# A vision tower with routed experts on one core: routed rows added to the output in memory, four late blocks worked between the units

## The reference, cut to what matters

```python
h = h + conv(layernorm(h))                      # residual h, 12608 tokens x 192
x = layernorm(h)
probs = softmax(x @ router_w)                   # 8 experts
gates, idx = top_k(probs, 2); gates /= sum(gates)
g = silu(x @ w_gate[e]);  u = x @ w_up[e]       # expert e, hidden width 192
routed = sum over the token's two experts of gate * ((g * u) @ w_down[e])
shared = (silu(x @ ws_gate) * (x @ ws_up)) @ ws_down     # hidden width 768
alpha = sigmoid(x @ sg_w + sg_b)
out = h + alpha * shared + (1 - alpha) * routed
```

## Time and profile before

| | us |
|---|---|
| median of 3 runs | 1256.18 (1250.46 to 1256.38) |
| the profiled execution | 1252.63 |
| its span, first to last instruction | 1250.80 |
| shared stage, first chunk to the next stage | 326.5 to 777 |
| units, first matmul to the last scatter | 782.4 to 1137.4 |
| `finish`, first transfer to the end | 1147.0 to 1250.8 |

### The profile page before, as it was taken

One profiled execution on the slowest core, in us unless ns is written; L12 is line 12 of the kernel. 1 busy time (PEld: TensorE's weight loads), 2 busy tenths in 40 slices (PEclk: granted clock), 3 DMA queues, 4 the chain that ended last, 5 costly groups with the idle time before them and its releaser, 6 DMA issues. The chain is left out here.

```text
span 1250.8 us, 24364 instructions
## 1 busy us (share of the span) xinstructions
PE 1040.9 (83%) x7867; PEld 718.1 (57%) x7868; DVE 868.9 (69%) x2637; ACT 537.4 (43%) x1023; POOL 656.7 (53%) x682
## 2 busy tenths in 40 slices
PE   5977997684599998999999996888878878864997
PEld 5967886684365655656666663444444445432555
DVE  6999776322487788888788765566666666651998
ACT  1233533222455555555556541444444444431332
POOL 0134413000377776777777752376766776763543
PEclk9989999788699999999999998899999999996999
DMA  8678786866995435454333216565555555333997
GB/s 298 239 238 268 231 257 161 212 132 172 203 211 148 123 90 135 121 129 97 93 87 97 69 49 184 117 126 111 129 113 118 123 115 135 94 86 112 306 299 241
DMA packets 285967, 196.08 MB, mean 157 GB/s; under 512 B 178840, under 2 KB 264602, under 8 KB 285590
## 3 DMA queue, kind: packets, MB, share of 16 engines
q1 hardware_dynamic: 251152, 142.46, 44.6%
q0 software_dynamic: 19488, 39.17, 9.3%
q10 hardware_dynamic: 15206, 12.93, 4.0%
HBM read 100.52 MB, written 74.65 MB: 140 GB/s over the span
## 5 line engine op out<-in xcount | busy, mean ns | idle before, releaser
L1728 POOL DMA_INDIRECT parts<-unit_yu,unit_token x208 | 215.9, 1038 | 97.2 <-issue 47.4
L1310 POOL DMA_INDIRECT routed<-rows_w,slot x198 | 216.6, 1094 | 64.1 <-issue 64.1
L1492 DVE SCALAR_TENSOR_TENSOR hf<-psu,sg 128x512 f32<-128x512 f32 x120 | 82.8, 690 | 83.8 <-ACT sg L1233 40.3
L1160 PE MATMUL pso<-ffn_w_hi,hh 128*128 128x192 f16 x480 | 119.4, 249 | 23.0 <-DVE hl L1497 18.0
L1233 ACT ACTIVATE sg<-psg 128x512 f32<-128x512 f32 x120 | 71.8, 599 | 147.3 <-PE psg L1145 114.2
L454 POOL TENSOR_TENSOR e_rs<-e_ve,mhalf 98x8 f32<-98x8 f32 x16 | 49.8, 3114 | 138.3 <-DVE e_ve L692 131.4
L1160 PE MATMUL pso<-ffn_w_hi,hl 128*128 128x192 f16 x480 | 119.2, 248 | 0.3 <-issue 0.3
L1160 PE MATMUL pso<-ffn_w_lo,hh 128*128 128x192 f16 x480 | 119.1, 248 | 0.0
L1145 PE MATMUL psg<-xt,ffn_w_hi 128*128 128x512 f16 x360 | 118.9, 385 | 0.0
L1145 PE MATMUL psu<-xt,ffn_w_hi 128*128 128x512 f16 x360 | 118.0, 382 | 0.3 <-issue 0.3
L524 PE MATMUL ps<-w,area 128*98 128x192 f32 x528 | 99.9, 333 | 0.0
(11 more groups left out here) (245 smaller groups left out, 2817.9 us busy)
## 6 DMA issues: line engine op xcount, KB each, us to landing
end_part<-parts SPq DMA_DIRECT2D x48, 384.0 KB, 5.6
area<-in_xa_dram SPq DMA_DIRECT2D x33, 392.0 KB, 5.5
area<-in_xb_dram SPq DMA_DIRECT2D x33, 392.0 KB, 6.2
resid<-spare ACTq DMA_DIRECT2D x32, 294.0 KB
hin<-resid SPq DMA_DIRECT2D x24, 384.0 KB
yin<-mixed SPq DMA_DIRECT2D x96, 96.0 KB
spare<-in_xa_dram SPq DMA_DIRECT2D x15, 392.0 KB, 6.1
spare<-in_xb_dram SPq DMA_DIRECT2D x15, 392.0 KB, 7.6
```

What stands on the lines that cost most here:

```text
L1160: last = nc.tensor.matmul(o, hx[m % 2][:, ts], wd[k][:, m], start=(a == 0 and m == 0 and t % 2 == 0), stop=(a == 2 and m == NSH - 1), skip ...
L1310: nc.gpsimd.indirect_dma_start(out=routed[:, :], out_offset=bass.IndirectOffsetOnAxis(ap=slot[q][:, k, t:t + 1], axis=0), in_=rows_w[q][:, ...
L1492: nc.vector.scalar_tensor_tensor(out=hf[i][:], in0=psu[:, i], scalar=1.0 / SCALE, in1=sg[i][:], op0=ALU.mult, op1=ALU.mult).then_inc(s["hf ...
L1728: nc.gpsimd.indirect_dma_start(out=parts[:, :], out_offset=bass.IndirectOffsetOnAxis(ap=token[q][:, k:k + 1], axis=0), in_=y[q][:, k, :], ...
```

## The change

- `NLATE` is 4: 21 blocks get their shared part in `shared_expert`, 126 chunks, and `PACE` is 5 for each period and 6 for the last.
- The last four blocks' chunks are worked in `routed_experts` as 48 half chunks (256 tokens, 128 hidden columns), one "guest" with each of the 48 written-out units: `guest_up` between `up(i)` and `down(i-1)`, `guest_down` after `down(i-1)`. Their results stay in `sums`.
- `lay`: SP stores each block's `sums` to `out` during `shared_expert` (for the four late blocks the residual alone). 14 of these stores stand between the loads, 10 after them, the last (block 20) after the fillers.
- A unit's indirect DMAs go to `out` itself with an add. Rows of one expert's units never meet; rows of two experts can. So `unit_table` makes a third row of `units`: the number of the first unit of this unit's expert, plus one. SP counts units whose rows have landed (`landed`), after the load of the unit five further on, and `send` waits for the count that the table gives. The first send also waits for all `lay` stores.
- After the last unit GpSimd adds the four late blocks from `sums` to `out` with five plain DMAs that add. `parts` and `finish` are gone, and with them one of two small operations of `meta`.

```diff
--- before.py
+++ after.py
@@ -85,13 +85,20 @@
...
-NLATE = 5
+NLATE = 4
+HOSTED = 4
 NOW = NBLK - NLATE
-PACE = [5, 5, 4] * ((NBLK - 1) // 3) + [8]
+LATE = NOW + HOSTED
+PACE = [5] * (NBLK - 1) + [6]
 XR = 8
 MAX_UNITS = 2 * NTOK // UNIT + E
 MIN_UNITS = -(-2 * NTOK // UNIT)
 STRAIGHT = MIN_UNITS - 2
+HALVES = 2 * HOSTED
+GUESTS = NSH * HALVES
+GUEST_OF = {i: i for i in range(GUESTS)}
+NLAID = NBLK + 1
+HB = BT // 2
...
@@ -1068,6 +1078,22 @@
...
+            def lay(b):
+
+                if b < NOW:
+                    sp.wait_ge(s["out_ready"], 2 * (b + 1))
+                else:
+                    sp.wait_ge(s["h2_ready"], b + 1)
+                sums = sums_of(t, b, tiles(b))
+                if b < NBLK - 1:
+                    sp.dma_start(rows(out, b, NT), sums).then_inc(late["laid"], 16)
+                else:
+                    at = (NBLK - 1) * BT
+                    mid = LAST_START + 128
+                    sp.dma_start(out[at:mid], sums[at - LAST_START:128, 0]).then_inc(late["laid"], 16)
+                    sp.dma_start(out[mid:NTOK].rearrange("(t p) d -> p t d", p=128),
+                                 sums[:, 1:]).then_inc(late["laid"], 16)
...
@@ -1083,7 +1109,13 @@
...
+                if LAG <= b < LAG + EASY:
+                    lay(b - LAG)
+
+            for b in range(NOW, NBLK):
+                lay(b)
+            for b in range(EASY, NOW - 1):
+                lay(b)
...
@@ -1095,6 +1127,7 @@
...
+            lay(NOW - 1)
             sp.wait_ge(s["fillers"], 16 * (NFILL + 1 + E))
...
@@ -1469,6 +1502,9 @@
...
+                step(nc.vector.tensor_tensor(gj[:], ge[:], start[:].unsqueeze(1).to_broadcast(shape), ALU.mult))
+                step(nc.vector.tensor_reduce(firstf, gj[:], op=ALU.max, axis=X))
+                nc.vector.tensor_scalar(t["units"][:, 2], firstf, 1.0, None, ALU.add)
...
@@ -1609,8 +1651,18 @@
...
+        def guest(i):
+
+            return GUEST_OF.get(i) if isinstance(i, int) else None
+
+        def guest_place(j):
+
+            half, m = divmod(j, NSH)
+            b, side = NOW + half // 2, half % 2
+            return b, side, m, min(NT // 2, tiles(b) - side * NT // 2)
...
@@ -1630,7 +1682,31 @@
...
-            schedule(n, sp, load)
+            def land(q, value):
+
+                sp.wait_ge(s[f"sent{q}"], value)
+                sp.sem_inc(late["landed"], 1)
+
+            def sent_by(i):
+
+                return 32 * (i - i % 2) + 64
+
+            sp.sem_inc(late["landed"], 1)
+            for i in range(STRAIGHT):
+                load(i, i % 2, i % XB, 16 * (i // XB + 1))
+                if i >= BEHIND:
+                    land((i - BEHIND) % 2, sent_by(i - BEHIND))
+            land((STRAIGHT - BEHIND) % 2, sent_by(STRAIGHT - BEHIND))
+            with nc.sync.Fori(0, n - STRAIGHT // 2) as j:
+                for i in range(2):
+                    load(2 * j + (STRAIGHT + i), i, i, None)
+                for i in range(2):
+                    land(i, 64 * j + sent_by(STRAIGHT - 4))
+            more = nc.sync.value_load(t["pairs"][0:1, 0:1], min_val=MIN_UNITS // 2 - 1, max_val=(MAX_UNITS + 1) // 2 - 1)
+            for i in range(2):
+                land(i, 64 * more)
+            for i in range(2):
+                land(i, 64 * n)
...
@@ -1670,12 +1746,41 @@
...
+            def guest_up(j):
+                b, side, m, nt = guest_place(j)
+                cols, ts = slice(m * 128, (m + 1) * 128), slice(side * HB, side * HB + nt * 128)
+                if j >= 2:
+                    pe.wait_ge(late["hf_ready"], j - 1)
+                for k in range(2):
+                    prods = ((wa[0], 0), (wa[1], 0), (wa[0], 2), (wb[0], 1), (wb[1], 1))
+                    for a, (wt, x) in enumerate(prods):
+                        last = nc.tensor.matmul(gps[:, j % 2, k * HB:k * HB + nt * 128], wt[:, k, cols],
+                                                t["xt"][b % XR][:, x, ts], start=(a == 0), stop=(a == 4))
+                last.then_inc(late["g_ps"], 1)
+
+            def guest_down(j):
+                b, side, m, nt = guest_place(j)
+                pe.wait_ge(late["hl_ready"], j + 1)
+                if m == 0 and j:
+                    pe.wait_ge(late["out_ready"], j // NSH)
+                for k in range(nt):
+                    for a, (hx, r) in enumerate(((hhx, 0), (hhx, 1), (hlx, 0))):
+                        last = nc.tensor.matmul(gpo[:, k * D:(k + 1) * D], hx[j % 2][:, k * 128:(k + 1) * 128],
+                                                wd[r][:, m], start=(a == 0 and m == 0 and k == 0),
+                                                stop=(a == 2 and m == NSH - 1), skip_group_check=True)
+                last.then_inc(late["down_ps"], 1)
+
             def body(i, q, k, landed):
                 up(i, k, landed)
+                if guest(i) is not None:
+                    guest_up(guest(i))
                 if not (isinstance(i, int) and i == 0):
                     down(i - 1, 1 - q)
+                if isinstance(i, int) and guest(i - 1) is not None:
+                    guest_down(guest(i - 1))
 
             schedule(n, pe, body)
...
@@ -1703,8 +1808,21 @@
...
+                j = guest(i)
+                if j is not None:
+                    act.wait_ge(late["g_ps"], j + 1)
+                    if j >= 2:
+                        act.wait_ge(late["hf_ready"], j - 1)
+                    nj = guest_place(j)[3] * 128
+                    nc.scalar.activation(sgx[j % 2][:, 0:nj], gps[:, j % 2, 0:nj], ACT.Silu,
+                                         scale=1.0 / SCALE).then_inc(late["sg_ready"], 1)
                 if not (isinstance(i, int) and i == 0):
                     y_out(i - 1, 1 - q)
+                if j is not None:
+                    act.wait_ge(late["hf_ready"], j + 1)
+                    if j >= 2:
+                        act.wait_ge(late["down_ps"], j - 1)
+                    nc.scalar.copy(hhx[j % 2][:, 0:nj], hfx[j % 2][:, 0:nj]).then_inc(late["hh_ready"], 1)
...
@@ -1718,6 +1836,9 @@
...
                 pool.wait_ge(s["y_d"], i + 1)
+                if isinstance(i, int) and i == 0:
+                    pool.wait_ge(late["laid"], 16 * NLAID)
+                pool.wait_ge(late["landed"], table(nc.gpsimd, 2, i))
...
@@ -1726,13 +1847,12 @@
...
                     nc.gpsimd.indirect_dma_start(
-                        out=parts[:, :], out_offset=bass.IndirectOffsetOnAxis(ap=token[q][:, k:k + 1], axis=0),
-                        in_=y[q][:, k, :], in_offset=None, bounds_check=2 * NTOK - 1,
-                        oob_is_err=False).then_inc(s[f"sent{q}"], 16)
+                        out=out[:, :], out_offset=bass.IndirectOffsetOnAxis(ap=token[q][:, k:k + 1], axis=0),
+                        in_=y[q][:, k, :], in_offset=None, bounds_check=NTOK - 1,
+                        oob_is_err=False, compute_op=ALU.add).then_inc(s[f"sent{q}"], 16)
 
             nc.gpsimd.memset(const[:], 0.0).then_inc(s["const_ready"], 1)
-            nc.gpsimd.memset(span[:], float(NTOK)).then_inc(s["const_ready"], 1)
-            pool.wait_ge(s["const_ready"], 2)
+            pool.wait_ge(s["const_ready"], 1)
...
@@ -1740,8 +1860,21 @@
...
             send(2 * n - 1, 1)
-            for q in range(2):
-                pool.wait_ge(s[f"sent{q}"], 64 * n)
+            pool.wait_ge(late["landed"], 2 * n + 1)
+            pool.wait_ge(late["out_ready"], HALVES)
+            wait(pool, "turn", 2 * n)
+            nc.gpsimd.tensor_tensor(carry[:], const[:], const[:], ALU.add).then_inc(s["turn"], 1)
+            for b in range(NOW, NBLK):
+                sums, at = sums_of(t, b, tiles(b)), b * BT
+                if b == NBLK - 1:
+                    mid = LAST_START + 128
+                    nc.gpsimd.dma_start(out[at:mid], sums[at - LAST_START:128, 0],
+                                        accum_op=ALU.add).then_inc(late["added"], 16)
+                    sums, at = sums[:, 1:], mid
+                end = min(NTOK, (b + 1) * BT)
+                nc.gpsimd.dma_start(out[at:end].rearrange("(t p) d -> p t d", p=128), sums,
+                                    accum_op=ALU.add).then_inc(late["added"], 16)
+            pool.wait_ge(late["added"], 16 * (HOSTED + 1))
...
@@ -1753,16 +1886,13 @@
...
-                nc.vector.scalar_tensor_tensor(out=shift[:].unsqueeze(2), in0=first, scalar=expert,
-                                               in1=span[:].unsqueeze(2), op0=ALU.is_equal,
-                                               op1=ALU.mult).then_inc(s["parts_ready"], 1)
...
-                dve.wait_ge(s["parts_ready"], 2 * i + 2)
...
-                nc.vector.tensor_tensor(token[q][:].unsqueeze(2), shift[:].unsqueeze(2), word[:, :, 0:1], ALU.add)
+                nc.vector.tensor_copy(token[q][:].unsqueeze(2), word[:, :, 0:1])
...
@@ -1775,8 +1905,20 @@
...
+            def guest_out(j):
+                b, side, m, nt = guest_place(j)
+                if m < NSH - 1:
+                    return
```

(42 more changed lines are left out.)

170 lines of the change are left out of this document (10 added, 160 removed).

## The result

The changed kernel takes 1246.25 us (median of 12 runs, 1241.63 to 1250.59), the kernel before in the same session 1253.66 (12 runs, 1247.94 to 1258.08): ratio 0.9952, interval 0.9934 to 0.9970. That is 7 us or 0.5% faster, where 1213, 3.2% less, was forecast. The forecast is 33 us too low.

The account below looks back on a forecast made before the run. The prediction took TensorE to bound the shared stage, the units' engines to wait for each other, and DMA and TensorE to be near full in `finish`. Span 1250.8 + 18 + 37 - 96 = 1210, forecast 1213, range 1178 to 1275.

Parts of the forecast that it names:

- +18 forecast: Shared stage: six more chunks lengthen it by 18 us, between +8 and +25; periods +20, its last period -2.
- +20 was forecast for the periods: Shared stage's 24 full periods: eight more chunks at 3.15 us, +25, less 0.6 us in each of eight periods.
- as long as a scatter that adds is issued as fast as one that writes: Units: condition for GpSimd's 6.3 us a unit staying below TensorE's floor of 6.7; the forecast pitch was 7.2, +37 us.
- the bounds from nothing to three times: Units' adding scatters: cost nothing more than writes (0.98 us issue, 2.0 landing, 0.276 of all engines), or two to three times that.
- the prediction's own sign of being wrong: Units: the prediction is wrong if a single adding scatter costs 0.4 us more to issue, or gates stop the loads.
- rival A: Units: GpSimd's issue becomes the bound; at 1.47 us per adding scatter, pitch 8.3 and time 1267, slower; chance 0.18.
- a fixed part: Units: GpSimd's 6.3 us a unit, 5.7 plus 0.6 for the table load and its use, without four scatters of 0.98.
- At most 14 us, mostly within GpSimd's slack: Units: seven waits for landing at expert changes, 0.4 us late each, 2 with slower landing; counted within 0.5 us of waits.
- the prediction's estimate with a 2 us slower read of memory: Units: with 2 us for an add's memory read at high load, the seven gates 2.4 us late, 17 us in all.
- Guests: Units: 1.58 us of TensorE work each fills its waits; pitch 7.2 for 6.43, +37 us, bounds +15 to +80.
- 40.9: End: microseconds from last `up` to the end, instead of 136.6, without the gap and `finish`: -96 (-102 to -88).
- rival E: End: the work of `finish` doesn't leave; five adding DMAs cost 40 us, time 1241, still faster; chance 0.05.

Follow-up runs that it names:

- the experiment: The changed kernel with scatters adding to an array with a place for every row, without the wait for `landed` in `send`: 1221.92 us, ratio 1.0215, 14 us under the changed kernel.

## Why the prediction was wrong, step by step

The span is 1245.9 for 1210, +35.8: shared stage -7.4, units +30.8, end +12.4.

- **Shared stage.** +18 forecast, +10.7 measured at the first `up` (793.07 for 782.42), inside the range of 8 to 25. VectorE's table starts 13.6 us later than before (768.40 for 754.81) where +20 was forecast for the periods, and from there to the first `up` it is 24.7 us for 27.6 (-2 forecast). The fillers do end the stage: VectorE's last operation ends at 784.97 and the last filler's issue at 784.35, but the first load follows only at 789.17. Whether the `lay` stores made the fillers land later wasn't tried.
- **The step that failed: "as long as a scatter that adds is issued as fast as one that writes".** It was written as a condition and then taken as met, and the bounds from nothing to three times were applied to the DMA engines' time and to landing, not to GpSimd's own time to issue. That went from 0.98 to 1.58 us, x1.6, and so past the prediction's own sign of being wrong, 0.4 us more. The pitch became 7.83 for 7.2, and this, with the gates in it, is +30.8 over 51 pitches. It is rival A, to which 0.18 was given.
- **Rival A's own number was too high,** 1267, and 1290 by its formula with the true g. Its cycle had a fixed part of 6.3 - 4 x 0.98 = 2.4 us; measured it is 7.67 - 4 x 1.58 = 1.35. The table load, counted at 0.6, runs in the queue while a scatter is worked on, as `carry` does, whose row starts before the scatter ahead of it has ended: the load in front of the send of 857.18 stands at 852.6, for 0.30 us, beside the scatter of 851.55 to 853.09. With the fixed part as it was counted the pitch would have been 8.7 and the kernel slower on the first chip too.
- **Gates.** "At most 14 us, mostly within GpSimd's slack": 17 in the profile, 14 by the experiment, and nothing of it in slack, since GpSimd has none. The amount was right, its cover wasn't. That each gate costs 2.4 us, as the prediction's estimate with a 2 us slower read of memory has it, is luck: behind the last send an adding scatter lands only 0.6 us later than a writing one, and the rest is the whole wait for landing, of which it had counted 0.4 us as exposed.
- **Landing** of the last adding scatter takes 1.96 us (1225.8 to 1227.77). The prediction had 2.0 for the writing ones too, read from a start of VectorE that was waiting for "remote", which may have been `down` and not the rows; behind the last send a writing scatter's rows are counted after 1.35. The DMA engines' share went by the upper of the two bounds, x3.0. As forecast, neither binds.
- **Guests** hide, as forecast, but behind GpSimd and not in TensorE's own gaps; TensorE is at 87% and the clock at 0.94, not over 90% and 0.97.
- **The end,** 53.3 us for 40.9. GpSimd is 33.2 us behind the last `up`, not 26.2 (+7.0); landing and count took 2.0 for 2.7; the five adding DMAs 11.7 for 12, so rival E is out. The remaining 6.4 are the `DRAIN` (6.0) and what follows it. The 9.6 us gap was said to go with `finish`; 7.9 of it were the `DRAIN` at the end of the units, and this stage still has one.
- **What bounds the kernel now** was misread in one place. The remote waits of the earlier trace rows were put down to the landing of rows. GpSimd's are waits for a result of TensorE, which by that profile comes 2 to 4 us late, and at 965 us ScalarE and VectorE wait for the same one; no profile of another chip has any. The units of before lose 40 us to waiting that no other chip has. The pitch of 6.43 against which the guests were priced was thus partly such a wait; on the other chips the pitch before is 5.6, the guests and the adds push it to 7.8, and the change loses 3.3%.

No version that computes the whole output beats the kernel before on the three other chips: six late blocks give back 12 us of the 40, and the gates' 14 can't be had while two experts' rows may meet. Kept open: whether the late results made both shared stages longer on the first chip, why one chip delivers TensorE's results late, or only marks them so, and why the changed kernel's units don't show it there.

## What to carry to other kernels

Price a DMA that GpSimd starts in two currencies, the DMA engines' time and the engine's own time to issue, and put the bounds of an unknown on both. If an engine's queue of work is at 89% of the pitch, a price that is unknown on that queue is the forecast's first term, not its rival. Before comparing with a pitch, look whether waits in it name nothing in the program; if so, measure the kernel before on a second chip.

## What the runs showed of the hardware

- An indirect DMA of 128 rows takes GpSimd 0.98 us to issue when it writes and 1.55 when it adds. The 1.55 holds for rows of 384 and of 768 bytes, with 0.60 to 0.78 of the DMA engines' time taken, and for the first scatter (1.60) after 20 us without one.
- Five plain DMAs of 1.43 MB take it 6.1 us to issue when they add and 3.7 when they store.
- In DMA time the adding one costs 3 times the writing one (0.82 to 0.276 us of all 16 engines); behind the last send its rows are counted 1.96 us after its end, a writing one's 1.35.
- At the end of the units GpSimd's queue has a `DRAIN` after its last DMA has landed: 7.9 us in the kernel before (on two chips), 6.0 in the changed one (on three), 5.6 in the kernel before with adding scatters, 4.6 with writing ones and 1.0 with six late blocks. What sets it wasn't tried.
- One and the same program ran at 1254 us on one chip and at 1195.5 to 1197.2 on three others.
